# One scan over 1024 tokens in place of two scans of 512 in a state-space layer

## The reference

```python
delta = softplus(x @ Wd + bd)
Bm = x @ WB + bB
Cm = x @ WC + bC
A = -exp(A_log)
def step(h, inps):
    x_t, d_t, B_t, C_t = inps
    bar_A = exp(minimum(d_t[:, :, None] * A, 2.0))
    bar_B = clip(d_t[:, :, None] * B_t[:, None, :], -2.0, 2.0)
    h = clip(bar_A * h + bar_B * x_t[:, :, None], -100.0, 100.0)
    y = sum(h * C_t[:, None, :], axis=-1) + x_t * D_param
```

## Time and profile before

| | us |
|---|---|
| median of 3 runs | 919.48 |
| lowest and highest run | 915.9, 922.57 |
| profiled execution, span from its first to its last instruction | 920.4 |
| PE busy | 640.0 |
| DVE busy | 715.4 |
| ACT busy | 537.6 |
| POOL busy | 566.2 |

### The profile page before, as it was taken

The page is one execution under the profiler, slowest core; times in us unless marked ns, Lnnn a source line. Parts: engine busy times, 40 slices in busy tenths (PEclk is TensorE's granted clock), DMA queues, the critical chain, the costliest instruction groups (busy, mean ns, idle before and its releaser), DMA issues.

```text
span 920.4 us, 14199 instructions
## 1 busy us (share of the span) xinstructions
PE 640.0 (70%) x4263; PEld 511.3 (56%) x4322; DVE 715.4 (78%) x1458; ACT 537.6 (58%) x988; POOL 566.2 (62%) x452
## 2 busy tenths in 40 slices
PE   3466658783799658973899379865896399638755
PEld 1234436672587437862778258743885277517624
DVE  3699897689988998799979998899879986432152
ACT  5373273664785749583876478565955276226422
POOL 1366548657964887568766787488747873562151
PEclk9576676996799869995999689986998599859968
DMA  3333344775367536754576536862574457325400
GB/s 102 128 127 115 138 149 148 243 225 189 112 218 237 197 96 190 239 166 153 163 243 202 188 113 219 247 203 85 203 240 138 156 166 247 89 82 154 135 23 24
DMA packets 82087, 149.31 MB, mean 162 GB/s; under 512 B 9404, under 2 KB 51144, under 8 KB 81992
## 3 DMA queue, kind: packets, MB, share of 16 engines
q1 hardware_dynamic: 69192, 135.13, 45.2%
q0 software_dynamic: 4096, 8.40, 2.8%
q10 hardware_dynamic: 8704, 4.72, 1.9%
HBM read 132.80 MB, written 15.40 MB: 161 GB/s over the span
## 4 chain that ended last, share of the span: by engine, by line
PE 30%; DVE 26%; issue 15%; ACT 15%; DMA 7%; POOL 4%; SPq 1%; another core or an unknown queue 0%; ACTq 0%; DVEq 0%; POOLq 0%
DVE state L1218 12%; DMA weights<-in_w_pack 5%; PE psY L561 4%; PE psU L691 4%; DVE psB L1209 4%; PE psD L585 4%; ACT hid L846 4%; PE psT L705 3%; ACT decay L807 3%; PE psU L732 2%; PE psU L734 2%; DVE bst L1152 2%; PE psB L555 2%; ACT L846 2%; PE psU L619 1%
## 5 line engine op out<-in xcount | busy, mean ns | idle before, releaser
L1245 POOL TENSOR_TENSOR prod<-state,c_wide 128x1024 f32<-128x1024 f32 x128 | 308.4, 2415 | 149.1 <-DVE state L1218 127.3
L1209 DVE TENSOR_TENSOR psB<-dx,psB 128x512 f32<-128x512 f32 x256 | 166.7, 689 | 31.6 <-PE psB L555 13.7
L1218 DVE TENSOR_TENSOR_SCAN state<-decay,state,psB 128x512 f32<-128x512 f32 x128 | 163.8, 1280 | 14.0
L555 PE MATMUL psB<-parts,sel 128*128 128x512 bf16 x198 | 89.5, 466 | 122.4 <-DVE state L1218 121.1
L1218 DVE TENSOR_TENSOR_SCAN state<-decay,psB 128x512 f32<-128x512 f32 x128 | 155.4, 1214 | 3.2 <-ACT decay L807 3.2
L561 PE MATMUL psY<-ident,prod 128*128 128x128 f32 x1024 | 155.0, 305 | 1.1 <-DVE state L1218 0.5
L807 ACT ACTIVATE decay<-delta,a_sb 128x1024 f32<-128x1024 f32 x128 | 142.0, 1141 | 15.7 <-DVE state L1218 7.4
L561 PEld LDWEIGHTS psY<-ident,prod 128*128 128x128 f32 x1024 | 137.5, 159 | 12.3 <-issue 7.9
L555 PEld LDWEIGHTS psB<-parts,sel 128*128 128x128 bf16 x256 | 25.8, 103 | 174.2 <-DVE state L1218 168.1
L846 ACT ACTIVATE hid<-psU,weights 128x128 f32<-128x128 f32 x352 | 99.7, 371 | 39.2 <-PE psU L691 33.7
L691 PE MATMUL psU<-yT_sorted,weights 128*128 128x128 f32 x704 | 96.1, 282 | 19.4 <-DMA weights<-in_w_pack 8.3
(11 more groups left out here) (165 smaller groups left out, 1080.4 us busy)
## 6 DMA issues: line engine op xcount, KB each, us to landing
c_wide<-c_rows SPq DMA_DIRECT2D x128, 512.0 KB, 5.2
weights<-in_w_pack SPq DMA_DIRECT2D x88, 514.0 KB, 4.2
xT_sb<-in_xT SPq DMA_DIRECT2D x8, 512.0 KB, 5.0
y_sorted<-rows_in SPq DMA_DIRECT2D x16, 256.0 KB, 3.1
xt<-in_x SPq DMA_DIRECT2D x8, 512.0 KB, 4.4
rows_out<-result SPq DMA_DIRECT2D x16, 256.0 KB, 4.3
out<-x ACTq DMA_DIRECT2D x16, 256.0 KB, 2.5
y_sorted<-rows_in SPq DMA_DIRECT2D x8, 192.0 KB, 4.5
```

Of the source, the lines that this page charges most:

```text
L555: pe.matmul(tokens(psB, c, h), sel[:, s, :], parts[:, c.n % 2, h * HALF:h * HALF + c.hw], start=True, stop=True).then_inc(b_ready, 1)
L1209: v.tensor_tensor(tokens(psB, c, h), dx[:, n % 2, h * HALF:h * HALF + c.hw], tokens(psB, c, h), ALU.mult).then_inc(inp_ready, 1)
L1218: v.tensor_tensor_scan(state[:, g % NSTATE, t0:t0 + c.hw], decay[:, g % NDECAY, t0:t0 + c.hw], tokens(psB, c, h), before, ALU.mult, ALU.ad ...
L1245: g_.tensor_tensor(prod[:, g % NPROD, w], state[:, g % NSTATE, w], c_wide[:, g % NC, w], ALU.mult).then_inc(prod_ready, 1)
```

## The change

The two scans of a state become one scan over 1024 columns of `psB`, and the semaphore between them goes. The products stay two instructions. The scan waits for both products, and both spreads of the next state wait for `state_ready`.

```diff
@@ spread_b, PE
-                p = c if s > 0 else CHUNKS[c.n - 1]
-                if h == 0 and g > 0 and p.halves == 2:
-                    pe.wait_ge(first_scanned, c.twos0 + s if s > 0 else p.twos0 + S)
-                else:
-                    wait(pe, state_ready, g)
+                wait(pe, state_ready, g)
@@ run, DVE
                         dve.wait_ge(decay_ready, g + 1)
-                        for h in range(c.halves):
-                            t0 = h * HALF
-                            before = state[:, g % NSTATE, t0 - 1:t0] if h else carry[:, s:s + 1] if c.follows else 0.0
-                            dve.wait_ge(inp_ready, spreads + h + 1)
-                            if h:
-                                dve.wait_ge(first_scanned, c.twos0 + s + 1)
-                            v.tensor_tensor_scan(state[:, g % NSTATE, t0:t0 + c.hw], decay[:, g % NDECAY, t0:t0 + c.hw],
-                                                 tokens(psB, c, h), before, ALU.mult, ALU.add
-                                                 ).then_inc(first_scanned if h + 1 < c.halves else state_ready, 1)
+                        dve.wait_ge(inp_ready, spreads + c.halves)
+                        v.tensor_tensor_scan(state[:, g % NSTATE, 0:c.w], decay[:, g % NDECAY, 0:c.w], psB[:, 0:c.w],
+                                             carry[:, s:s + 1] if c.follows else 0.0, ALU.mult, ALU.add
+                                             ).then_inc(state_ready, 1)
```

More of the change, by code:

```diff
@@ L54, in __init__ @@
         self.halves0 = p.halves0 + p.halves if p else 0
-        self.twos0 = p.twos0 + S * (p.halves == 2) if p else 0
         self.blocks0 = p.blocks0 + p.blocks if p else 0
@@ L403, in ssm_moe_ffn_kernel @@
         state_ready = sem("state_ready")
-        first_scanned = sem("first_scanned")
         prod_ready = sem("prod_ready")
@@ L1009, in slow_scan @@
                     step(bass.ds(t, 1), st[:, bass.ds(t - 1, 1)])
-                if c.halves == 2:
-                    v.tensor_copy(st[:, 0:1], st[:, 0:1]).then_inc(first_scanned, 1)
                 v.tensor_copy(st[:, c.w - 1:c.w], st[:, c.w - 1:c.w]).then_inc(state_ready, 1)
```

## The result

The changed kernel takes 938.5 us (median of four runs, 935.29 to 941.76) against 920.48 for the kernel before (four runs, 915.9 to 922.57). The ratio is 1.0192, 95% interval 1.0161 to 1.0223: slower, by about three times what the prediction said, and outside its range. In the profiled executions the span grew from 920.4 to 933.5 us, 13.1 us.

The account below looks back on a forecast made before the run. DVE was taken to bound each period's front half and PE the back half. The start +3.1, six back halves +6.0 and six front halves −3.0 gave +6.1 us on the median 919.48: 925.6 us, range 917 to 934.

Parts of the forecast that it names:

- Step 2: Rest of the second chunk: hangs on GpSimd's scatters and expert weight transfers, so put at zero.
- Step 1: Start, 34 to 128 us, 20 states: ten without cover +3.9, state 3 +0.9, nine others −1.7; sum +3.1 us.
- covered state: State with another DVE task before the next state: shorter time from first product to state's end saves 0.19 us.
- uncovered one: State following its predecessor directly on DVE: next spread waits for the whole scan, costing about 0.39 us.
- Step 3: Six back halves, chunks 2 to 7: PE stalls 1.0 us before state 15's first spread, delaying the next chunk; +6.0 us.
- Step 4: Six front halves: savings at state 0 and covered states outweigh costs at states 1 and 2; −0.5 each, −3.0 us.
- the long scan is no cheaper than two: Rival, every scan on the path: long scan takes 2.49 us, +13.6 us more, total 939.2; chance 0.12.
- The fixed cost once per state: Faster rival, every state: one fixed cost less, spread's wait hidden, only savings stay; −11.5 us, 908.0; chance 0.06.
- the stall at state 15 is hidden: Rival, back halves: waits behind PE's stall (weights, banks) hide it; +0.1 us, 919.6; chance 0.16.
- More stalls on PE at state 9: Rival, state 9: second spread and all behind it 0.75 late, +4.5 us more, 930.1; chance 0.14.

Follow-up runs that it names:

- e1: The changed kernel, with POOL's prod 6 of the second chunk waiting until the third chunk's delta is done; 934.36 us, ratio 1.0164.
- e5: The changed kernel, with POOL's prod 7 (not 6) of the second chunk waiting for the third chunk's delta; one run, 934.8 us.
- e7: The kernel before, old scans and waits, with the third chunk's delta waiting for prod 6 of the second chunk; one run, 930.41 us against 922.6.
- e4: The changed kernel with prod 6 waiting for delta and state 15's first spread moved behind FFN part and down projection; 926.93 us, ratio 1.0046.
- e3: The changed kernel, with the first spread of state 15 moved behind the last FFN part and an expert's down projection; 932.92 us, ratio 1.011.
- e2: The kernel before, keeping two scans, with both spreads of a state waiting for state_ready; 950.88 us, ratio 1.0311.
- e6: The kernel before, with one long scan only where DVE has another task behind the state, two scans elsewhere; 914.44 us, ratio 0.9927.

## Why the prediction was wrong

By its own steps, with the distances of the profiled executions:

| step | forecast | measured |
|---|---|---|
| 1, the start, to the second chunk's slots | +3.1 | +3.5 |
| 2, the rest of the second chunk | 0 | +7.6 |
| 3 and 4, five of the six periods | +2.5 | +2.7 |
| from the eighth chunk's state 0 to the end | +0.5 | −0.7 |
| sum | +6.1 | +13.1 |

(After minus before in the table of ends: 3.49; 11.10 − 3.49; 13.76 − 11.10; 13.1 − 13.76.)

**Step 2 failed.** It said that the rest of the second chunk "hangs on GpSimd's scatters and on the transfers of expert weights" and put it at zero. That was right of the kernel before, where the turn of the sorted rows waits for their transfer (150.24). The sorted rows came 2.4 us later (their issue moved from 147.55 to 149.98), but the turn came 10.8 later, since it stands in PE's queue behind the spread of state 9, which waits for the scan of state 8, which stands behind `delta`. I looked only at who waits for whom by semaphore, and no semaphore holds `delta` there; e1, e5 and e7 show that it waits for POOL's pause. With `delta` free the zero was near: in this stretch e1 and e4 move by −1.5 and −0.3 against before. The rows that warn of it were in the trace of before: the scatter of 2.02 us beside `delta`, and in each of the six middle periods a `combine` of 2.9 to 3.2 us, against 1.14 elsewhere, that meets one `prod`. One of the six, behind one of usual length; DVE:

```profile
411.96 1.14 DVE L1134 SCALAR_TENSOR_TENSOR moe<-chosen_out,top_w,ytok 128x128 f32<-128x128 f32 x4
...
432.75 3.17 DVE L1134 SCALAR_TENSOR_TENSOR moe<-chosen_out,top_w,ytok 128x128 f32<-128x128 f32 x4
```

POOL:

```profile
432.55 2.37 POOL L1245 TENSOR_TENSOR prod<-state,c_wide 128x1024 f32<-128x1024 f32 x1
```

It ends at 435.92, 1.00 after the `prod` (434.92).

**Step 1** came out near in size, +3.5 against +3.1, partly by luck. The scan starts 0.10 after the end of the second product and not 0.04: I had taken 0.04 from a pair in which the scan needed only the first product (80.13), so it shows no wait. That makes a covered state save 0.11 in place of 0.19 and an uncovered one cost 0.47 in place of 0.39. Ten uncovered states and five covered ones are worth +0.8 and +0.4 by this. Against it, the other four covered states (7, 10, 11 and 13 of the first chunk) took 3.94 to 4.00 before, not the 3.80 that I had put for all, so they saved some 0.3 each, −0.4 in all. These sizes give +3.9, and one pair of executions does not tell that from +3.5.

**Step 3** was right: 0.98 us of idle PE, 0.9 for each period by e3. **Step 4** was too good: without the stall five periods take 496.0 to 496.9 (e3, e4) against 497.1 and 497.8 (before, e7), 1.0 less, or 0.2 for each period in place of 0.5. So the +2.7 of the table, near the forecast +2.5, is again partly luck: it rests on one execution, and the four traces with the stall, 501.1 in the mean, are 4.0 above before.

**The rivals.** That the long scan is no cheaper than two (939.2) fell: its record is 2.287, and e2 with the short scans is slower still. That the rival's time lies near the measured one is chance. The fixed cost once per state is real (2.494 − 2.287 = 0.207 us), but the time went the other way. That the stall at state 15 is hidden (919.6) fell with e3. More stalls on PE at state 9 were not needed to explain the sum: PE's loads do wait 0.97 us there (461.14), but before they stood idle for 1.56 at the same place (449.16), and now for 0.55 behind the wait.

That `delta` and POOL get in each other's way had a rule: the Trainium skill, "SBUF — State Buffer", section "Who interferes with whom", says that a VectorE instruction with two SBUF inputs contends with a GpSimd instruction that reads SBUF, and that issue order decides which one blocks. The traces agree on who is hit (`delta`, `combine`) and who is not (the products and scans with `psB`), and on a swap of roles: 2.02 us for the scatter in before, 8.23 for `delta` in after. They differ in two things. The blocked instruction did not wait for one instruction of POOL but for all three of a row. And by the records `delta` began first, 0.40 us ahead of the `prod` that held it (148.32 and 148.72). In later chunks the same order of starts goes the other way. DVE, then POOL, in the kernel before:

```profile
338.40 1.22 DVE L1025 SCALAR_TENSOR_TENSOR delta<-zb,sp 128x1024 f32<-128x1024 f32 x1
```

```profile
338.63 1.05 POOL L1283 TENSOR_TENSOR ve<-mv,eps 128x4 f32<-128x4 f32 x1
```

Here `ve` began 0.23 behind `delta` and stood still until it was over, 1.05 us in place of its usual 0.20. So the order of starts in the profile does not tell which of the two is held; what settles it was not tried.

## What to carry to other kernels

When an edit shifts one engine against another by even 2 us, go through the instructions of VectorE that read two SBUF operands and see which rows of GpSimd's tensor instructions they will newly meet; a record far over its group's usual length, or a scatter of double length, marks the places. Here fusing two instructions paid only where the successor is covered, since the first half's early release was hiding a handover of 0.48 us: apply it state by state, as e6 does. Where a wait must fall on one of two engines, put it on the one behind which less waits: 0.66 us of wait on GpSimd gave back over 6.

## What the runs showed of the hardware

- A VectorE instruction of 1.20 us with both operands in SBUF stood still through three, two and one GpSimd tensor instructions in a row, and ended 1.09 to 1.10 us after the last of them (8.23, 5.36 and 3.87 us long in after, e7 and e5). There is no semaphore wait and no idle time in the profile: the engine counts as busy.
- A scatter that had begun 0.33 us before did not hold it (e1), while a scatter that began 0.01 us after it took 2.02 us in place of 0.96 (before). A GpSimd instruction of 0.20 us that began 0.23 us after it took 1.05 (before, 338.63).
- A scan of 1024 columns takes 2287 ns where one of 512 takes 1214: 1073 ns for the second 512 columns, so some 141 ns are fixed, if the time grows evenly with the columns.
